# The impulse's second sum and its two small steps go one place further down VectorE's program; on the DMA queue their store and loads go behind that group's other two transfers

## What is computed

```python
def step(s, xt):
    s = jnp.einsum('bdn,dnm->bdm', s, A) + xt[..., None] * Bp
    y = jnp.einsum('bdn,dn->bd', s, Cp) + Dp * xt
    return (s, y)
s0 = jnp.zeros((Bsz, D, N), xg.dtype)
_, ys = jax.lax.scan(step, s0, jnp.moveaxis(xg, 1, 0))
```

## Time and profile before

| | |
|---|---|
| median of 3 runs | 490.37 us (490.25 to 492.69) |
| the profiled execution, its own time | 489.83 us |
| its span, from the first to the last instruction | 488.0 us |
| granted TensorE clock, mean | 0.996 |
| PE busy | 96% of the span |
| VectorE busy | 82% |
| ScalarE, GpSimd busy | 74%, 70% |

### The profile page before, as it was taken

The page is one execution under the profiler, slowest core; times in us unless marked ns, Lnnn a source line. Parts: engine busy times, 40 slices in busy tenths (PEclk is TensorE's granted clock), DMA queues, the critical chain, the costliest instruction groups (busy, mean ns, idle before and its releaser), DMA issues. The chain is left out here.

```text
span 488.0 us, 13769 instructions
## 1 busy us (share of the span) xinstructions
PE 467.5 (96%) x4405; PEld 403.8 (83%) x4405; DVE 398.0 (82%) x1212; ACT 361.5 (74%) x880; POOL 340.3 (70%) x446
## 2 busy tenths in 40 slices
PE   8899999999999999999999898887999999999995
PEld 6688888989888898898988787776888888888885
DVE  2988888889889888899888876788769788797654
ACT  3787777878878878788787786656697786876752
POOL 2488997868667677776876766125789887887563
PEclk9999999999999999999999999999899999999999
DMA  7945647758757566674764747684021312301102
GB/s 258 316 151 161 217 155 195 223 155 241 184 148 229 145 194 186 164 218 140 230 171 142 192 120 164 144 259 130 0 57 32 87 43 45 87 6 39 44 1 88
DMA packets 77172, 70.29 MB, mean 144 GB/s; under 512 B 39319, under 2 KB 59948, under 8 KB 76588
## 3 DMA queue, kind: packets, MB, share of 16 engines
q1 hardware_dynamic: 77100, 69.41, 49.6%
HBM read 56.74 MB, written 12.65 MB: 142 GB/s over the span
## 5 line engine op out<-in xcount | busy, mean ns | idle before, releaser
L1958 POOL TENSOR_TENSOR sq_lo<-fc_in,sq_hi 128x512 fp32r<-128x512 f32 x63 | 82.7, 1315 | 29.3 <-ACT sq_hi L1909 29.3
L1041 ACT COPY ctxT<-turn_ps 128x512 f32<-128x512 f32 x128 | 68.9, 590 | 9.1 <-PE turn_ps L802 3.1
L1901 ACT ACTIVATE relu<-fc_ps,fc_square 128x512 f32<-128x512 f32 x64 | 43.8, 686 | 30.9 <-PE fc_ps L1820 30.8
L2003 DVE SCALAR_TENSOR_TENSOR fc_in<-fc_ps,relu 128x512 f32<-128x512 f32 x64 | 43.7, 685 | 26.4 <-ACT relu L1901 25.6
L1236 POOL TENSOR_TENSOR hb_lo<-hbT,hb_hi 128x256 fp32r<-128x256 f32 x32 | 23.9, 747 | 42.6 <-ACT hb_hi L1120 42.6
L1222 POOL TENSOR_TENSOR rstd<-ve,neg_half 128x1 f32<-128x1 f32 x64 | 35.1, 553 | 25.5 <-DVE ve L1511 18.4
L1814 PE MATMUL fc_ps<-xn_hi,fc_T 128*128 128x512 f32 x128 | 52.1, 407 | 0.5 <-DVE fc_in L2003 0.5
L1814 PE MATMUL fc_ps<-xn_lo,fc_T 128*128 128x512 f32 x128 | 50.9, 398 | 0.0
L1228 POOL TENSOR_TENSOR proj_in<-proj_in,below 128x512 f32<-128x512 f32 x31 | 48.1, 1552 | 0.0
L802 PE MATMUL turn_ps<-ident,ctxn 128*128 128x128 f32 x352 | 47.5, 278 | 0.0
L1837 PEld LDWEIGHTS proj_ps<-proj_T,sq_hi 128*128 128x128 f32 x252 | 38.8, 189 | 5.4
(11 more groups left out here) (261 smaller groups left out, 1449.5 us busy)
## 6 DMA issues: line engine op xcount, KB each, us to landing
ctxn<-in_ctx SPq DMA_DIRECT2D x22, 1024.0 KB, 5.5
toeplitz<-in_ctx SPq DMA_DIRECT2D x10, 1024.0 KB, 5.5
resid<-in_x SPq DMA_DIRECT2D x32, 128.0 KB, 5.4
ctx_end<-in_ctx SPq DMA_DIRECT2D x32, 128.0 KB
gated_tokens<-gated SPq DMA_DIRECT2D x32, 128.0 KB, 5.9
scan_x<-gated_tokens SPq DMA_DIRECT2D x60, 64.0 KB, 4.8
out<-resid SPq DMA_DIRECT2D x7, 512.0 KB, 3.2
scan_quarters<-scan_x SPq DMA_DIRECT2D x3, 1024.0 KB, 6.0
```

What stands on the lines that cost most here:

```text
L1041: act.copy(ctxT[:, b, :, 0:J - 1], turn_ps[b % 2][:, :].rearrange("p (k j) -> p k j", k=KD)).then_inc(ctxT_copied, 1)
L1901: act.activation(relu[m % 2], fc_ps[m % 2][:, :], ACT.Relu, scale=fc_square[:, m:m + 1]).then_inc(relu_done, 1)
L1958: pool.tensor_tensor(sq_lo[:, tile(c, m) % PARTS, :], sq[m % SQ], sq_hi[:, tile(c, m) % PARTS, :].bitcast(F32), ALU.subtract).then_inc(sq_ ...
L2003: dve.scalar_tensor_tensor(out=sq[m % SQ], in0=fc_ps[m % 2][:, :], scalar=0.0, in1=relu[m % 2], op0=ALU.max, op1=ALU.mult).then_inc(sq_don ...
```

## The change

On VectorE `impulse_sums(1)` and `impulse_response()` stood at the end of step 29. They now stand in the middle of step 30, behind `weights(30)` and ahead of `dot1(31)`. On SyncE `step(29)` is issued first, and only then the impulse's store and the first windows. Nothing is added or taken away.

```diff
                     if base >= 4:
                         scan_load_pair(base)
+                    step(base + 1, 0, ())
                     if base + 1 == LAST_STATE + 1:
                         sp.wait_ge(imp_steps, IMPULSE)
                         sp.dma_start(impulse_dram.rearrange("(c p) l -> p c l", p=P), impulse[:, :, :]).then_inc(impulse_stored, 16)
                         sp.wait_ge(impulse_stored, 16)
                         for q in range(NB):
                             windows_load(q, 0)
-                    step(base + 1, 0, ())
...
                     weights(g)
+                    if g == LAST_STATE + 2:
+                        impulse_sums(1)
+                        impulse_response()
                     if g + 1 < GROUPS:
                         dot1(g + 1)
...
-                    if g == LAST_STATE + 1:
-                        impulse_sums(1)
-                        impulse_response()
```

## The result

The changed kernel has a median of 492.37 us (491.13 to 495.5) where the kernel before has 490.77 in the same comparison (19 of its 20 executions lie between 489.35 and 493.02; one took 2554 us and doesn't move the median). The ratio is 1.0034, with a 95% interval of 1.0021 to 1.0048. I forecast 490.6 and "within 0.5%". The second held. The time lies above my range of 489.2 to 491.8, also if the ratio is applied to the 490.37 that I forecast from (492.04). The change costs 1.67 us (1.0 to 2.4) where I had 0.3.

A forecast was written before the change was run, and what follows sets the result against it. The prediction took VectorE's program in step 30 as the bound, with TensorE waiting for it. From 490.37 us, 1.26 off, 1.26 back, +0.28 for L1447 and +0 for the windows gave 490.65, rounded to 490.6; range 489.2 to 491.8.

The forecast's parts named there:

- What the move takes away: VectorE, end of step 29: without the three impulse instructions, everything behind moves forward 1.26 us.
- the first stall: TensorE's 1.08 us idle ahead of the turn of z in step 30, forecast to go nearly altogether.
- Where it comes back: VectorE, step 30 ahead of dot1: the block takes 1.26 us again, TensorE waits longer ahead of sum_gate, gain zero.
- The new neighbours: VectorE's L1447 in step 30 waits for GpSimd's add_beta, taking 0.68 us instead of 0.40, so +0.28 us.
- The windows: Window loads land at 286.7; GpSimd's place_high waits 0.4 us, within 0.68 us of slack, so +0.
- a rival for it: Impulse's store lands late behind other transfers, windows late, up to 494.3 us; chance 0.15 up to 2 us, 0.05 more.
- its smaller form: Windows 0.5 to 1 us later than estimated, giving 490.9 to 491.6 us; chance 0.15 for up to 2 us.
- The sum: Whole kernel: 1.26 us taken away, 1.26 put back, +0.28 for L1447, +0 for windows, giving 490.65, rounded to 490.6.

The follow-up runs named there:

- dve_pool: Changed kernel with SyncE's old order put back and GpSimd's place_high(2, 0) moved behind hcq_lo in step 31; ratio to the kernel before 1.0039.
- dve_only: Changed kernel with SyncE's old order put back, so only VectorE's move remains; ratio to the kernel before 1.0032.
- pool_later: Changed kernel with GpSimd's place_high(2, 0) moved behind hcq_lo in step 31; ratio to the kernel before 1.0020.
- weights_later: Kernel before with impulse block behind hq in step 30, L178 taken to step 31, and GpSimd's place_high(2, 0) behind hcq_lo; ratio 1.0011.
- fill12_pool: Changed kernel with 12 extra TensorE transposes ahead of sum_gate of step 30 and GpSimd's place_high(2, 0) behind hcq_lo in step 31; ratio 1.0008.
- fill12: Changed kernel with 12 extra TensorE transposes ahead of sum_gate of step 30; ratio to the kernel before 1.0025.
- fill12_old: Changed kernel with SyncE's old order put back and 12 extra TensorE transposes ahead of sum_gate of step 30; ratio to the kernel before 1.0018.
- late_block: Kernel before with the impulse block moved behind hq_lo in step 30 and GpSimd's place_high(2, 0) behind hcq_lo; ratio 1.0116.

## Why the prediction was wrong

- **What the move takes away: right.** 1.26 us off `nmr` and `hc`, and the first stall went.
- **Where it comes back: right in order and size, wrong in its price.** The step that failed is "TensorE arrives there earlier and waits longer [...] The stall is moved by a few instructions and not removed [...] The gain is zero". It took two short stretches (1.08 and 0.25 us) and one long one (1.79) as equal in price. Behind the long one the clock fell in two of the four traces that have it (the changed kernel and `dve_pool`, not `dve_only` and `pool_later`), for 1.5 us each. It fell in step 30 in none of the ten other traces, three of which have work in the stretch. In the first blocks of all 14 traces, up to 310 us, it fell five times: behind stretches of 1.79, 1.80, 1.93, 2.35 and 2.45 us. Behind those of 1.43 us and less there it didn't fall at all, also where the 1.43 us came in one piece (`weights_later`). So it isn't the joining alone that costs. In the second block the clock also fell behind a stretch of 1.49 us, in two traces of 14.
- **What the clock costs on average is less sure.** Over 24 executions with the stretch and no wait for the windows (`pool_later`, `dve_pool`) the mean time was 492.23 us, over 12 with the stretch filled (`fill12_pool`) 491.03, and over 28 of the kernel before 490.76, all in one comparison. So the filling is worth 1.2 us (0.7 to 1.7; `dve_pool` has SyncE's old order besides), and the 0.27 that are left (-0.2 to 0.7) fit VectorE's 0.29. The three pairs that differ in the filling alone (changed kernel and `fill12`, `pool_later` and `fill12_pool`, `dve_only` and `fill12_old`) give less by their ratios, 0.09, 0.12 and 0.14%, so 0.4 to 0.7 us, and by their medians -0.02, 0.24 and 0.00%. The mean clocks (0.9950 over 35 executions with the filling, 0.9925 over 56 with the stretch) agree in direction, but `fill12_pool` with 0.9956 is above the kernel before with 0.9944 too, so they hold more than the falls of step 30.
- **The new neighbours: right.** L1447 took 0.68 us, and the place costs 0.29 us in each trace without a fall.
- **The windows: mis-sized.** The term was 0, from one trace's 2.04 us for the store and 7.0 for the loads, with 0.28 us of slack left. Measured were 1.6 to 4.4 for the store and 7.0 to 9.0 for the loads, the latter in `fill12`, where the second half's loads start at 285.06 with the first not landed. In the changed kernel the store went out at 277.68 by the clock of the kernel before (278.25 - 0.57), as forecast; the first load came 1.1 us later than forecast, and the reader could start 2.0 us later than my 286.7. I had a rival for it and gave its smaller form 0.15, though the sum stood within 0.3 us of the point where it begins to cost. Its price by the ratios of the pairs that differ in GpSimd's slack alone is 0.14% (changed kernel and `pool_later`) and 0.17% (`fill12` and `fill12_pool`), so 0.7 to 0.8 us; the medians give -0.04 and 0.21%. The third such pair, `dve_only` and `dve_pool`, has SyncE's old order, and there the slack gained nothing (-0.07%), as its trace, in which TensorE never waits for the windows, leads one to expect.
- **The sum.** 0.3 for VectorE, 0.4 to 1.2 for the clock, and 0 to 0.8 for the windows hold the measured 1.67 us, but they don't test it. The chain of ratios from the changed kernel over `fill12` to `fill12_pool` (0.09 and 0.17%, with 0.08% left) adds up to 0.34% whatever the causes. What is shown is that with both repairs the loss is nearly gone, and that each mechanism is there in traces. VectorE's move alone costs as much as the full change (1.0032 and 1.0034), which speaks for the clock as the larger part.

On the loads, the Trainium skill (DMA: Bandwidth & Descriptors, section Two DMAs through the same engine are not ordered) says that transfers on the same engines overlap and that only the completion semaphore orders them. The traces agree that loads overlap: the four of `windows_load` start within 1.3 us and land 7 us and more behind the first of them, and in `fill12` those of the second half start at 285.06, 4.2 us ahead of the first half's reader. That this overlap is what made them late, no run isolates.

What stays open: why the same stretch lets the clock fall in one execution and not in the next. The second block has one of 2.5 us in all 14 traces (it ends at 339.70 in that of the kernel before), and the clock fell behind it in ten of them. In the changed kernel's trace the fall at 328 stands behind one of 1.49 us, and all 14 traces have one of 1.5 to 1.7 us at that place, with a fall in two (this one and `late_block`). Open are also the split between clock and windows, how much of the windows' lateness in the changed kernel is the order of the queue (between `fill12` and `fill12_old` there is 0.07%, which is no difference), and whether the extra fall in the second block of the traced execution has anything to do with the change.

## What to carry to other kernels

When a move only shifts a stall of TensorE, look at how the idle time is then laid out: two short waits joined into one can cost more than their sum, since the clock may fall behind a long one, as here behind 1.8 us in some executions and not behind 1.43 in the trace that has it. When a moved step starts a chain of DMAs, treat durations from one trace as one draw from a spread, and if the slack left is smaller than their spread, count the wait as likely. Moving small VectorE instructions next to GpSimd ones can use up the gain, as in `weights_later`. And before adding up the differences of runs as terms, see whether they would add up to the total in any case.

## What the runs showed of the hardware that I had not expected

- A single idle stretch of TensorE of 1.8 to 2.5 us in the first block was followed by the lower clock in five of seven traces (about 1.5 us lost behind one of 1.8); stretches of 1.0 to 1.4 us there never were, also two of 1.1 and 1.4 us within 4 us of each other.
- From the issue of a 64 KB store to the first load behind it, which waits for the store to have landed, passed 4.4 us with a 128 KB store issued 0.5 us ahead of it (one trace), 2.4 to 3.2 us with one 1.7 us ahead (four traces), and 1.6 to 2.6 us with none right ahead (nine traces).
- A `tensor_scalar` with one SBUF input (128x64) took 0.69 us beside a GpSimd instruction in both `weights_later` kernels, 0.81 us in `late_block` (279.68 to 280.49, while GpSimd's fill of `toeplitz` ran until 280.44), and 0.20 us where GpSimd's had just ended (at 272.33 in the trace of the kernel before, at 278.03 in that of the changed one).
